# Right sides of the landmark solve: heads spread over TensorE's four column groups, one PSUM bank and one copy a tile, four smaller stores in place of one

## The reference

```python
landmarks = K[:, :, landmark_idx, :]
Phi_K = jnp.exp(-_sq_dists(K, landmarks) / temperature)
Z = jnp.einsum('bhnk,bhnd->bhkd', Phi_K, V)
Y = jnp.linalg.solve(W_kernel, Z)
Phi_K_sum = jnp.sum(Phi_K, axis=-2)[..., None]
norm = jnp.einsum('bhnk,bhko->bhno', Phi_Q, jnp.linalg.solve(W_kernel, Phi_K_sum))
out = out_unnorm / norm
```

## Time and profile before

| | us |
|---|---|
| runs of the kernel | 4694.56, 4668.89, 4682.25 (median 4682.25) |
| the profiled execution | 4693.21 |
| its span | 4691.4 |
| the eight chunks of the stage (first distance matmul to the last store's issue) | 1649.7 to 1843.5 |
| from there to the first load of the next stage | 1843.5 to 1852.8 |

### The profile page before, as it was taken

One profiled execution on the slowest core, in us unless ns is written; L12 is line 12 of the kernel. 1 busy time (PEld: TensorE's weight loads), 2 busy tenths in 40 slices (PEclk: granted clock), 3 DMA queues, 4 the chain that ended last, 5 costly groups with the idle time before them and its releaser, 6 DMA issues. The chain is left out here.

```text
span 4691.4 us, 85272 instructions
## 1 busy us (share of the span) xinstructions
PE 3805.9 (81%) x30810; PEld 2831.4 (60%) x30810; DVE 2774.1 (59%) x5424; ACT 2084.6 (44%) x4510; POOL 875.2 (19%) x840
## 2 busy tenths in 40 slices
PE   7999999999999585279998679899995257869376
PEld 5777878777787354166666356566663135646254
DVE  2555555555555675442223776577777946877783
ACT  2333333333333354544333444378887535654423
POOL 0000000000000131210001036555551022200360
PEclk7999999999999787589998779999997578989667
DMA  3111111111111035220000023222220000000000
GB/s 76 43 55 41 50 46 45 46 45 53 42 50 46 13 113 183 87 100 0 0 0 20 5 114 124 82 72 65 74 65 17 0 5 3 0 13 0 8 2 23
DMA packets 189000, 214.35 MB, mean 46 GB/s; under 512 B 19312, under 2 KB 176976, under 8 KB 181328
## 3 DMA queue, kind: packets, MB, share of 16 engines
q1 hardware_dynamic: 188752, 211.05, 14.4%
HBM read 183.68 MB, written 27.05 MB: 45 GB/s over the span
## 5 line engine op out<-in xcount | busy, mean ns | idle before, releaser
L3758 PE MATMUL c_psO<-c_pt,c_vc 128*128 128x512 f32 x1024 | 482.1, 593 | 2.5 <-ACT c_ot L3845 2.5
L3730 PE MATMUL c_psS<-c_kc,c_qt 128*128 128x257 f32 x2048 | 465.9, 380 | 0.9 <-issue 0.9
L3837 ACT ACTIVATE c_sc<-c_psS,c_mx 128x257 f32<-128x257 f32 x512 | 214.9, 472 | 484.9 <-DVE c_mx L3895 484.9
L3730 PEld LDWEIGHTS c_psS<-c_kc,c_qt 128*128 128x128 f32 x2048 | 381.2, 190 | 66.8 <-issue 17.4
L3884 DVE COPY c_qt<-c_psQ 128x512 f32<-128x512 f32 x248 | 170.5, 687 | 399.9 <-PE c_psQ L3715 399.9
L547 PEld LDWEIGHTS f_psY<-f_w_down,f_hT 128*128 128x128 f32 x2560 | 302.4, 192 | 64.1 <-issue 50.4
L590 ACT ACTIVATE f_hT<-f_psH,f_b_up 128x512 f32<-128x512 f32 x320 | 214.3, 688 | 283.8 <-PE f_psH L537 278.8
L3715 PEld LDWEIGHTS c_psQ<-XT,c_m 128*128 128x128 f32 x1984 | 260.1, 191 | 106.2 <-issue 104.4
L537 PE MATMUL f_psH<-f_xs,f_w_up 128*128 128x512 f32 x640 | 304.6, 612 | 18.3 <-ACT f_hT L590 18.2
L547 PE MATMUL f_psY<-f_w_down,f_hT 128*128 128x128 f32 x2560 | 305.4, 275 | 10.2 <-ACT f_hT L590 7.0
L2223 POOL TENSOR_TENSOR x_sc<-x_sc,x_rec 128x1156 f32<-128x1156 f32 x128 | 270.5, 2113 | 207.4 <-DVE x_rec L2489 207.4
(11 more groups left out here) (794 smaller groups left out, 7675.2 us busy)
## 6 DMA issues: line engine op xcount, KB each, us to landing
c_kc<-in_ctxT SPq DMA_DIRECT2D x128, 257.0 KB, 3.1
c_vc<-in_ctx SPq DMA_DIRECT2D x128, 256.0 KB
g_wide<-g_w_dram SPq DMA_DIRECT2D x32, 1024.0 KB, 8.0
x_kc<-in_ctxT SPq DMA_DIRECT2D x32, 512.0 KB, 4.2
x_vc<-in_ctx SPq DMA_DIRECT2D x64, 256.0 KB
l_k_dram<-l_dist SPq DMA_DIRECT2D x32, 256.0 KB, 3.5
l_q_dram<-l_turn SPq DMA_DIRECT2D x8, 1024.0 KB, 10.0
y_pt<-l_q_dram SPq DMA_DIRECT2D x8, 1024.0 KB, 7.2
```

The source lines that it names most:

```text
L3730: mm = pe.matmul(psS[:, r, 0:KEYS], qt[:, b // BT, half, b % BT, r * G:(r + 1) * G].rearrange("p h i -> p (h i)"), kc[:, b // 2 % 2, b % 2 ...
L3758: mm = pe.matmul(psO[:], vc[:, slot, c % 2, t, half * P:(half + 1) * P], pt[:, c % 2, t], start=(t == 0), stop=(t == 1))
L3837: act.activation(sc[:, b % 2, r, 0:KEYS], psS[:, r, 0:KEYS], ACT.Exp, bias=mx[:, b % 2, r:r + 1]).then_inc(exp_done, 1)
```

## The change

The 16 heads of a tile no longer all leave on partitions 0 to 31. Head `r * 4 + q` goes to partitions `32 r` to `32 r + 31`, in columns `q * 36` on. Consecutive matmuls take `r` = 0, 1, 2, 3 and so go to the four column groups in turn. A tile now fills 144 columns of one bank on 128 partitions, and the two banks of `psR` serve even and odd tiles, so that two tiles can be made ahead of any copy. One copy a tile (128 by 144) takes the place of two (32 by 288). The layout of `r_dram` is unchanged. So the store of a tile is cut into four, one for each 32 partitions, with contiguous pieces of 36 floats (144 bytes) where there were pieces of 144 floats (576 bytes).

```diff
-        rb = sb("l_rb", [S, TC, G, H16, V])
+        rb = sb("l_rb", [P, TC, G, G, V])
...
-                        for half in range(2):
-                            sp.wait_ge(right_read[half], i * TC + t + 1)
+                        sp.wait_ge(right_read, i * TC + t + 1)
                         at = home((i * TC + t) * BT)
-                        sp.dma_start(r_dram[at:at + 13:4].rearrange("b i c -> i b c"),
-                                     rb[:, t].rearrange("p b h d -> p b (h d)")).then_inc(r_stored[t], 16)
+                        for r in range(G):
+                            sp.dma_start(r_dram[at:at + 13:4, :, r * G * V:(r + 1) * G * V].rearrange("b i c -> i b c"),
+                                         rb[r * S:(r + 1) * S, t].rearrange("p b h d -> p b (h d)"))\
+                                .then_inc(r_stored[t], 16)
...
-                        for half in range(2):
-                            if i or t:
-
-                                pe.wait_ge(right_read[half], i * TC + t)
-                            for h in range(half * 8, half * 8 + 8):
-                                mm = pe.matmul(psR[0:S, half, h % 8 * G * V:(h % 8 + 1) * G * V],
-                                               dist[:, i % 2, h // G, t * G + h % G, :],
-                                               vm[:, t, h].rearrange("p b d -> p (b d)"), start=True, stop=True)
-                            mm.then_inc(right_done[half], 1)
+                        if i or t >= 2:
+
+                            pe.wait_ge(right_read, i * TC + t - 1)
+                        for q in range(G):
+                            for r in range(G):
+                                mm = pe.matmul(psR[r * S:(r + 1) * S, t % 2, q * G * V:(q + 1) * G * V],
+                                               dist[:, i % 2, r, t * G + q, :],
+                                               vm[:, t, r * G + q].rearrange("p b d -> p (b d)"), start=True, stop=True)
+                        mm.then_inc(right_done, 1)
...
-                            act.wait_ge(r_stored[t], i * 16)
-                        for half in range(2):
-                            act.wait_ge(right_done[half], i * TC + t + 1)
-                            act.activation(rb[:, t, :, half * 8:half * 8 + 8].rearrange("p b h d -> p h b d"),
-                                           psR[0:S, half, 0:8 * G * V].rearrange("p (h b d) -> p h b d", h=8, b=G),
-                                           ACT.Copy).then_inc(right_read[half], 1)
+                            act.wait_ge(r_stored[t], i * G * 16)
+                        act.wait_ge(right_done, i * TC + t + 1)
+                        act.activation(rb[:, t].rearrange("p b h d -> p h b d"),
+                                       psR[:, t % 2, 0:G * G * V].rearrange("p (h b d) -> p h b d", h=G, b=G),
+                                       ACT.Copy).then_inc(right_read, 1)
```

More of the change, by code:

```diff
@@ L2663, in kernel_matrices @@
         temp_ready = k.sem("l_temp_ready")
-        right_done = [k.sem(f"l_right{n}_done") for n in range(2)]
-        right_read = [k.sem(f"l_right{n}_read") for n in range(2)]
+        right_done = k.sem("l_right_done")
+        right_read = k.sem("l_right_read")
         k_stored = [k.sem(f"l_k{n}_stored") for n in range(2)]
@@ L2709, in _ @@
                 for t in range(TC):
-                    sp.wait_ge(r_stored[t], 16 * CHUNKS)
+                    sp.wait_ge(r_stored[t], 16 * G * CHUNKS)
             @block.tensor
@@ L2857, in mask_values @@
                     if i:
-                        for half in range(2):
-                            g.wait_ge(right_done[half], i * TC)
+                        g.wait_ge(right_done, i * TC)
                     for t in range(TC):
@@ L2908, in complete @@
                     if m == 0 and i >= 2:
-                        v.wait_ge(right_done[0], (i - 1) * TC)
-                        v.wait_ge(right_done[1], (i - 1) * TC)
+                        v.wait_ge(right_done, (i - 1) * TC)
                         v.wait_ge(k_stored[i % 2], i // 2 * TC * 16)
```

## The result

The changed kernel takes 4673.83 us (median of 20 runs) against 4687.89 us for the kernel before in the same sessions: a ratio of 0.9968, 95% interval 0.9959 to 0.9978. It is faster by 0.3%, less than the half per cent taken as the bound. One of the 20 runs of the changed kernel took 5441 us at a granted clock of 0.707; the ratio leaves it out. The profiled execution took 4674.74 us with a span of 4672.8, where before it was 4691.4: 18.6 us less.

The account below looks back on a forecast made before the run. No engine was full: a chain through several engines bound each chunk, with VectorE waiting 3.74 us for tokens behind TensorE's right sides. Periods -19.6 and stage's end +3 gave -16.6 us, so 4666 us against the median, range 4648 to 4688.

Parts of the forecast that it names:

- Matmuls, copies, start of the tokens: Right sides of each chunk: bursts of 0.65 and 1.08 us, copies of 0.30 us, tokens starting 4.65 us earlier.
- Rival A: Right sides on TensorE: column groups don't overlap, records stay at 59 and 38 ns, 4676 us; chance 0.08.
- What carries the gain: Right sides on TensorE: records fall from 59 and 38 ns to 16.8 and 10.2 at clock 0.50 and 1.00.
- The period's term: VectorE's tokens end earlier, so each of seven periods is 2.8 us shorter: -19.6 us in all (-16 to -26).
- The small stores in the loop: The 16 right-side stores a chunk are hidden in the seven periods and cost nothing there.
- The end: Stage's end: twelve more store issues ahead of the store of `turn`, partly won back, +3 us (0 to +8.7).
- The cover of 1.7 us for the store of `turn`: Middle chunk: that store lands at 1731.1, the transpose needing it comes at 1732.8; cover was 5.9 us before.
- a sign of being wrong: In the profile after, a wait before the transpose named for `q_stored` would speak against the prediction; no size given.
- Rival B: Store of `turn` delayed by 82 ns packets, the next transpose waits 1 us, 4675 to 4680 us; chance 0.10.
- rival C: Small stores saturate the DMA engines, binding from 118 ns a packet; at 150 ns 4714 us; chance 0.04.

Follow-up runs that it names:

- same_group: The changed kernel with the two inner loops of the right sides exchanged, four matmuls in a row to one column group: 4672.60 us, ratio to before 0.9971.
- one_ahead: The changed kernel with only one tile, not two, allowed ahead of the first copy: 4701.66 us, ratio to before 1.0036.

## Why the prediction was right or wrong

The time (4673.83 in 4648 to 4688, forecast 4666) and the verdict (within half a per cent) were right. Against before of the same sessions the gain was 14.1 us, forecast 16.6. That the sum fits so well is partly luck: several terms were off, with different signs.

- **Matmuls, copies, start of the tokens: right.** Bursts 0.77 and 1.19 us (forecast 0.65 and 1.08), copies 297 ns (0.30), tokens 4.62 us earlier against the exponential (4.65), their length 4.92 us (some 4.9), the clock back after 4.8 us (5.2). Rival A, no overlap of the groups, fell with it. The rule of the Trainium skill ("TensorEngine Tiling (Array Packing)", Instruction Overhead) of some 60 cycles a matmul was counted too high in the prediction: it took each record for a matmul, but two records are one matmul. A burst is 32 matmuls: 0.77 us are 24 ns each, 58 cycles at 2.4 GHz, which agrees with the rule, and 1.19 us are 37 ns, 45 cycles at 1.2 GHz, which is below it. In one column group a matmul takes twice that.
- **What carries the gain: read too narrowly.** I took 59 and 38 ns as the price of a record in one column group, where same_group shows 39 and 24; the rest was waits for copies. same_group, whose bursts are twice as long, loses only 2.9 of the 23.5 us that VectorE's step won over seven chunks. one_ahead, whose records are fast, loses 2 to 3 us a chunk of it ahead of its stalls. So the second tile ahead carries most.
- **The period's term was mis-sized, 2.8 where 3.0 to 3.4 was measured.** In the first settled chunk VectorE's step from the end of its right operand (1727.77) to its last token (1733.57) takes 5.80 us against 8.72 before, so 2.92 as worked out. In the next it takes 5.22 (1748.79 to 1754.01), 3.50 less. I had the clock low from the burst on. There it fell only behind the burst, so the tokens ended 5.84 us after the exponential and not 6.42. Seven periods at some 3.3 are about -23. They came out at 20.5 to 20.9 us, below the 21 to 21.5 that I had named.
- **Long periods: not looked into.** Before had two, after has one. 3.5 + 3.5 - 3.5 = some 3.5 us of the -26.4 are this. The range of 23.9 to 27.4 us stood ahead of the prediction, and I multiplied the one chunk that I had read by seven without asking for the reason. Shown, in one execution each: with the placements out of the loop the stalls over 1.6 us are gone in three kernels. Argued only: that an instruction packet waits on a DMA engine behind the 64 KB rows of the placement. The packets are there in chunks without a stall as well, and the one in the stalled stretch of before is too little to tell; the cause stays open.
- **The small stores in the loop: put at nothing.** In the kernel before, cutting them cost 22 us by the medians, with stalls of 2.5 to 5.4 us. With the placements behind the loop it cost 4.3 us a stage. What they cost inside the changed kernel no run shows.
- **The end: +3 where +5.2 was measured.** Its parts, each against before: the last placement comes 12.06 us after the last chunk's first right side, not 8.20 (+3.9), since the four stores of `dist` took 6.93 us to issue against 3.20; the 16 stores took 7.76 us against 1.96 (+5.8; forecast 5.9); from the issue of the store of `turn` to the next load 4.99 against 9.38 (-4.4; forecast up to -4.3). Both terms that I had were right; the delay of the stores of `dist` I had not counted, and had allowed a gain there instead.
- **The cover of 1.7 us for the store of `turn`: used up.** The transpose waited twice, 3.2 us in all, which I had named as a sign of being wrong. 0.53 us fell where TensorE's tokens ended VectorE's step anyway. The 2.67 us fell in the last chunk, and there the store of `turn` stood behind 16 others on the queue until 1824.54. Rival B's place was right, its mechanism wrong: over 1732 to 1733 only small packets move, 291 of them in a share of 0.244, so 0.244 x 16 us / 291 = 13 ns each, not 82, and far from rival C's 118. The Trainium skill ("DMA: Bandwidth & Descriptors", Specifications) says that transfers under 512 bytes are done as read-modify-write; these of 144 bytes show at most a small price for it, 0.09 ns a byte against 0.07 for those of 576.

## What to carry to other kernels

Before one chunk is multiplied by the number of chunks, list all the periods: two of six here were 3.5 us longer than the one that I had read, for another reason. When a wait on a copy shrinks, ask whether the gain is in the faster work or in how much work is queued ahead of the copy; exchanging two loops told it. And count the DMA queue in issue slots as well as in bytes: twelve small stores took 5.8 us at a place without cover, whatever their few bytes. In the kernel before the same cut went with stalls of TensorE that cost more than that, and these went away when the large transfers left the loop.

## What was not expected of the hardware

- TensorE stalls of 2.5 to 5.4 us named "issue", in kernels whose only difference is when large DMAs are under way; with those DMAs behind the loop the longest is 0.8 to 1.6 us. Why is open.
- Stores of 144-byte packets at some 13 ns each, against 41 ns for 576 bytes: a packet's time went nearly with its bytes, 0.07 to 0.09 ns a byte.
- After waits of 4.37 and 3.99 us, in neighbouring chunks, the second burst ran at clock 0.50 and at 1.00. In the second case the clock fell 0.9 us after TensorE had taken up work again, with tokens under way.
